# Cluster sums of an image from bf16 parts of x, and one product with ones per unit

## What is computed

```python
xn = x / max(norm(x, axis=1), EPS); cn = centroids / max(norm(centroids, axis=1), EPS)
idx = argmax(einsum('bchw,nc->bnhw', xn, cn), axis=1)
onehot = one_hot(idx, 40)
sum_x = einsum('bhwn,bchw->bnc', onehot, x)          # cluster sums of each image
count = sum(onehot, axis=(1, 2))
centroids_local = sum_x / maximum(count, 1.0)[..., None]
gathered = centroids_local[b, idx]                   # the mean of each position's cluster
delta = transpose(gathered) - x
alpha = exp(-mean(delta * delta, axis=1, keepdims=True))
y = x + alpha * delta
out = relu(einsum('oc,bchw->bohw', W, y) + b)
```

## Time and profile before

| | |
|---|---|
| median of 3 runs | 431.25 us (431.1 to 432.02) |
| the profiled execution | 431.4 us, span 429.6 us |
| TensorE (PE) busy | 422.2 us, 98% |
| VectorE (DVE) busy | 285.3 us, 66% |
| ScalarE (ACT) busy | 243.4 us, 57% |
| GpSimd (POOL) busy | 206.7 us, 48% |
| HBM | 48.40 MB read, 25.17 MB written |

### The profile page before, as it was taken

One profiled execution on the slowest core, in us unless ns is written; L12 is line 12 of the kernel. 1 busy time (PEld: TensorE's weight loads), 2 busy tenths in 40 slices (PEclk: granted clock), 3 DMA queues, 4 the chain that ended last, 5 costly groups with the idle time before them and its releaser, 6 DMA issues.

```text
span 429.6 us, 5789 instructions
## 1 busy us (share of the span) xinstructions
PE 422.2 (98%) x2134; PEld 296.0 (69%) x2134; DVE 285.3 (66%) x378; ACT 243.4 (57%) x329; POOL 206.7 (48%) x102
## 2 busy tenths in 40 slices
PE   8999999999999999999999999999999999999996
PEld 6744466775777667775867757776677758777785
DVE  2368979485776767495883857767674956787730
ACT  5665385566465673565754664656735657555541
POOL 2000665486284482674553862844826745424330
PEclk9999999999999999999999999999999999999999
DMA  8996298976577946859379665879463220222123
GB/s 275 309 291 122 56 261 219 274 218 166 143 244 185 226 168 164 215 149 256 99 198 265 169 175 142 242 182 229 163 170 125 98 99 0 98 99 98 49 112 134
DMA packets 70927, 73.94 MB, mean 172 GB/s; under 512 B 2724, under 2 KB 45732, under 8 KB 70900
## 3 DMA queue, kind: packets, MB, share of 16 engines
q1 hardware_dynamic: 70900, 73.58, 61.9%
HBM read 48.40 MB, written 25.17 MB: 171 GB/s over the span
## 4 chain that ended last, share of the span: by engine, by line
PE 95%; DVE 2%; ACT 1%; issue 1%; POOL 0%; POOLq 0%; DVEq 0%
PE main L797 20%; PE main L799 20%; PE main L798 20%; PE sump L740 10%; PE fa L700 9%; PE gat L771 5%; PE al L778 1%; PE fa L709 1%; PE al L779 1%; PE al L819 1%; PE fa L724 1%; PE main L840 1%; PE al L785 1%; PE gat L785 1%; PE gat L812 1%
## 5 line engine op out<-in xcount | busy, mean ns | idle before, releaser
L284 POOL TENSOR_TENSOR z<-z,x 128x1024 f32<-128x1024 f32 x42 | 99.3, 2384 | 147.1 <-DVE z L389 147.1
L797 PE MATMUL main<-yh,wh 128*128 128x512 f32 x376 | 152.5, 406 | 0.0
L799 PE MATMUL main<-yh,wl 128*128 128x512 f32 x376 | 147.0, 391 | 0.0
L798 PE MATMUL main<-yl,wh 128*128 128x512 f32 x376 | 146.7, 390 | 0.0
L291 POOL TENSOR_TENSOR yl<-z,yh 128x1024 fp32r<-128x1024 f32 x44 | 106.0, 2423 | 57.9 <-ACT yh L530 57.9
L369 DVE TENSOR_TENSOR z<-gat,x 128x1024 f32<-128x1024 f32 x46 | 56.2, 1221 | 91.1 <-PE gat L771 91.1
L538 ACT ACTIVATE o<-main,bcol 128x512 f32<-128x512 f32 x96 | 65.7, 686 | 82.8 <-PE main L799 82.8
L797 PEld LDWEIGHTS main<-yh,wh 128*128 128x128 f32 x376 | 70.7, 188 | 20.4 <-issue 4.6
L799 PEld LDWEIGHTS main<-yh,wl 128*128 128x128 f32 x376 | 70.6, 188 | 15.2
L798 PEld LDWEIGHTS main<-yl,wh 128*128 128x128 f32 x376 | 70.7, 188 | 14.3
L530 ACT ACTIVATE yh<-z 128x1024 fp32r<-128x1024 f32 x48 | 50.5, 1052 | 22.9 <-POOL z L284 21.9
(11 more groups left out here) (114 smaller groups left out, 325.5 us busy)
## 6 DMA issues: line engine op xcount, KB each, us to landing
x<-x SPq DMA_DIRECT2D x24, 1024.0 KB, 5.7
out<-o SPq DMA_DIRECT2D x23, 1024.0 KB, 4.8
xs<-x SPq DMA_DIRECT2D x84, 256.0 KB, 6.3
o<-w SPq DMA_DIRECT2D x1, 1024.0 KB, 12.3
out<-o SPq DMA_DIRECT2D x4, 256.0 KB, 2.1
sq<-centroids SPq DMA_DIRECT2D x2, 80.0 KB
bcol<-bias SPq DMA_DIRECT2D x1, 2.0 KB, 11.7
```

The lines of the kernel that those rows point to most:

```text
L284: pool.tensor_tensor(z, z, X[g // PARTS % 2][:, pair(h), span(g)], ALU.add).then_inc(y_pool, 1)
L797: t_.matmul(main[:, o % 2, :], WH[:, k, rows], YH[g % 2][:, k, :], start=(k == 0), stop=False)
L798: t_.matmul(main[:, o % 2, :], WH[:, k, rows], YL[g % 2][:, k, :], start=False, stop=False)
L799: last = t_.matmul(main[:, o % 2, :], WL[:, k, rows], YH[g % 2][:, k, :], start=False, stop=(k == KC - 1))
```

## The change

For images 2 to 7 (g >= 6), two of the three units of an image (g % 3 below SPLIT = 2) get their cluster sums in another way. x is written exactly as three bf16 parts: the upper halfword of XT; then GpSimd (`first_rest`) subtracts that from XT into a new buffer XR, whose upper halfword is the second part; VectorE (`second_rest`) subtracts this in turn and writes the result, in bf16, into XR's lower halfwords. TensorE takes 12 bf16 products with `oh3` in place of 4 float32 products with `oh`, so it waits for `oh3_done` and `rest2_done`. GpSimd issues `first_rest(g + 5)` after `low_half(g, 1)`, VectorE `second_rest(g + 3)` at the end of an iteration. The third unit and images 0 and 1 stay in float32.

The ones product becomes one: ScalarE copies the upper 64 partitions of `al` (`move_upper`), VectorE adds them to the lower 64 (`fold`), `high_sum` and `low_sum` work on 64 partitions and write the two halves of one buffer SHL, and TensorE multiplies it once. It now stands after the last block of convolve, ahead of the next gather, for every g (for g = 2 after a block of convolve); `exp(g - 1)` moves to the next iteration, behind `relu(g - 3, 3)`. `argmax` is cut into `best_sims` and `first_best`, `means` into `scale_means` and `high_means`, and the order of calls on VectorE and ScalarE changes around them. keep_busy goes from 9 to 6.

```diff
+def split(g):
+    return g >= 2 * PARTS and g % PARTS < SPLIT
...
+        XR = sb("xr", [P, SPLIT, TILES, C], F32)
...
-        SH = sb("sh", [P, UNIT], F32R)
-        SL = sb("sl", [P, UNIT], F32R)
+        upper_sum = sb("upper_sum", [LOW, UNIT], F32)
+        SHL = sb("shl", [P, UNIT], F32R)
...
+            def first_rest(g):
+                pool.wait_ge(tr_done, g - PARTS + 1)
+                xt = XT[:, g % PARTS, :, :]
+                pool.tensor_tensor(XR[:, g % PARTS, :, :].rearrange("p t c -> p (t c)"),
+                                   xt.rearrange("p t c -> p (t c)"), halfword(xt, 1), ALU.subtract
+                                   ).then_inc(rest1_done, 1)
...
                 low_half(g, 0)
                 low_half(g, 1)
+                if g + 5 < UNITS and split(g + 5):
+                    first_rest(g + 5)
...
+            def second_rest(g):
+                dve.wait_ge(rest1_done, splits(g))
+                xr = XR[:, g % PARTS, :, :]
+                v_.tensor_tensor(halfword(xr, 0), xr.rearrange("p t c -> p (t c)"), halfword(xr, 1), ALU.subtract
+                                 ).then_inc(rest2_done, 1)
...
+            def fold(g):
+                dve.wait_ge(upper_done, folded(g))
+                v_.tensor_tensor(al[0:LOW, :], upper_sum[:, :], al[0:LOW, :], ALU.add).then_inc(fold_done, 1)
...
                 add_squares(g)
-                if beside and p < 2:
+                if beside and p == 0:
                     transpose_half(g + 4, 1)
+                fold(g)
                 if beside and p == 2:
                     rest_of_mean(b + 1)
+                if beside and p == 1:
+                    best_sims(b + 1)
                 low_half(g - 1, 1)
                 low_sum(g)
                 if beside and p == 1:
-                    argmax(b + 1)
+                    first_best(b + 1)
+                    transpose_half(g + 4, 1)
                 if beside and p == 2:
                     parts_of_mean(b + 1)
                     if g + 4 < UNITS:
                         transpose_half(g + 4, 0)
                         transpose_half(g + 4, 1)
+                if g + 3 < UNITS and split(g + 3):
+                    second_rest(g + 3)
...
+            def move_upper(g):
+                act.wait_ge(s_done, folded(g))
+                a_.activation(upper_sum[:, :], al[LOW:P, :], ACT.Copy).then_inc(upper_done, 1)
...
                 b, p = divmod(g, PARTS)
                 beside = b + 1 < BATCH
+                relu(g - 3, 3)
                 if g > PARTS:
-                    relu(g - 3, 3)
+                    exp(g - 1)
                 square(g, 0)
...
                     high_half(g - 1, 1)
-                    means(b + 1)
                     relu(g - 2, 0)
+                    scale_means(b + 1)
+                    move_upper(g)
+                    high_means(b + 1)
                     high_sum(g)
                     relu(g - 2, 1)
...
+                    move_upper(g)
+                    high_half(g - 1, 1)
                     high_sum(g)
-                    high_half(g - 1, 1)
                     if beside:
                         relu(g - 2, 1)
                 relu(g - 2, 2)
-                exp(g)
                 if beside and p == 1:
                     copy_onehot(b + 1)
...
+                if split(PARTS * b + u):
+
+                    pe.wait_ge(oh3_done, b + 1)
+                    pe.wait_ge(rest2_done, splits(PARTS * b + u))
+                    for t in range(HALF):
+                        for i, x_part in enumerate((halfword(XT[:, u, :, :], 1), halfword(XR[:, u, :, :], 1),
+                                                    halfword(XR[:, u, :, :], 0))):
+                            for h in range(2):
+                                tile = HALF * h + t
+                                last = t_.matmul(sumP[NPAD * h:NPAD * (h + 1), :], oh3[:, slot(u, tile), 0:NPAD],
+                                                 x_part[:, tile * C:(tile + 1) * C],
+                                                 start=(u == 0 and t == 0 and i == 0), stop=False)
+                    last.then_inc(c_done, 1)
+                    return
...
-                t_.matmul(al[:, :], ones[:, :], SH[:, :], start=True, stop=False)
-                t_.matmul(al[:, :], ones[:, :], SL[:, :], start=False, stop=True).then_inc(one_done, 1)
+                t_.matmul(al[:, :], ones[:, :], SHL[:, :], start=True, stop=True).then_inc(one_done, 1)
...
-            keep_busy(9)
+            keep_busy(6)
...
                 convolve(g - LAG, 2)
-                if beside:
-                    sum_squares(g)
                 convolve(g - LAG, 3)
-                if not beside:
-                    sum_squares(g)
+                sum_squares(g)
```

More of the change, by code:

```diff
@@ L31 @@
 LAG = 2
+LOW = P // 2
 EPS = 1e-12
 TAIL = UNITS - 1 - PARTS
+SPLIT = 2
 DIRECT = 2
@@ L57, in made, with splits @@
     return by_vector, 2 * g + h + 1 - by_vector
+def split(g):
+    return g >= 2 * PARTS and g % PARTS < SPLIT
+def splits(g):
+    return sum(split(i) for i in range(g + 1))
 def folded(g):
@@ L153, in build @@
         pair_done, s_done, sh_done, sl_done = sem("pair_done"), sem("s_done"), sem("sh_done"), sem("sl_done")
+        rest1_done, rest2_done = sem("rest1_done"), sem("rest2_done")
+        upper_done, fold_done = sem("upper_done"), sem("fold_done")
         one_done, exp_done, za_done = sem("one_done"), sem("exp_done"), sem("za_done")
@@ L180, in squares, with halfword @@
             return SQ[:, :, :] if h == 0 else gat[:, :, :]
+        def halfword(words, which):
+            return words.rearrange("p t c -> p (t c)").bitcast(BF16).rearrange("p (c w) -> p c w", w=2)[:, :, which]
         def plain(b):
@@ L317, in transpose_half, with best_sims @@
                     last.then_inc(tr_done, 1)
-            def argmax(b):
-                shape = [P, PARTS * TILES, N]
+            def second_rest(g):
[3 more added lines that the diff above has]
+                                 ).then_inc(rest2_done, 1)
+            def best_sims(b):
                 dve.wait_ge(simT_done, b + 1)
@@ L323, in argmax, with first_best @@
                 v_.tensor_reduce(best[:, :], simT, AXIS_X, ALU.max).then_inc(arg_step, 1)
+            def first_best(b):
+                shape = [P, PARTS * TILES, N]
                 dve.wait_ge(arg_step, 4 * b + 1)
@@ L379, in add_squares @@
                 v_.tensor_tensor(al[:, :], SQ[:, 0, :], upper[:, 1, :], ALU.add).then_inc(s_done, 1)
+            def fold(g):
+                dve.wait_ge(upper_done, folded(g))
+                v_.tensor_tensor(al[0:LOW, :], upper_sum[:, :], al[0:LOW, :], ALU.add).then_inc(fold_done, 1)
             def low_sum(g):
                 dve.wait_ge(sh_done, folded(g))
-                wait(dve, one_done, g)
-                v_.tensor_tensor(SL[:, :], al[:, :], SH[:, :].bitcast(F32), ALU.subtract).then_inc(sl_done, 1)
+                v_.tensor_tensor(SHL[LOW:P, :], al[0:LOW, :], SHL[0:LOW, :].bitcast(F32), ALU.subtract
+                                 ).then_inc(sl_done, 1)
             def scale(g, h):
@@ L431, in _ @@
             keep_transposed()
-            argmax(0)
+            best_sims(0)
+            first_best(0)
             for k in range(KC):
@@ L444, in _ @@
                 delta(g, 1)
-            argmax(1)
+            best_sims(1)
+            first_best(1)
             scale(0, 0)
@@ L461, in _ @@
             rest_of_mean(1)
+            parts_of_mean(1)
+            fold(2)
             low_sum(2)
-            parts_of_mean(1)
             transpose_half(6, 0)
@@ L567, in copy_sums, with scale_means @@
                 a_.activation(sumsH[:, :], sumP[:, :], ACT.Copy).then_inc(sumsH_done, 1)
-            def means(b):
+            def scale_means(b):
                 act.wait_ge(rc_step, 2 * b + 2)
@@ L572, in means, with high_means @@
                 a_.activation(mean(b), mean(b), ACT.Copy, scale=rcount[:, :]).then_inc(mean_step, 1)
+            def high_means(b):
                 act.wait_ge(mean_step, 2 * b + 1)
@@ L607, in _ @@
             evacuate_onehot(0)
-            means(0)
+            scale_means(0)
+            high_means(0)
             act.wait_ge(b_in, 16)
@@ L628, in _ @@
             square(2, 1)
-            means(1)
+            scale_means(1)
+            high_means(1)
+            move_upper(2)
             high_half(1, 1)
@@ L632, in _ @@
             relu(0, 2)
-            relu(0, 3)
-            exp(2)
             for g in range(PARTS, UNITS):
@@ L652, in _ @@
                     relu(g - 2, 0)
+                    if g == PARTS:
+                        exp(g - 1)
                     square(g, 1)
@@ L670, in _ @@
             relu(g - 2, 3)
+            exp(g)
             relu(g - 1, 0)
@@ L894, in _ @@
             convolve(0, 3)
-            sum_squares(2)
             for g in range(PARTS, UNITS):
@@ L908, in _ @@
                     convolve(g - LAG, 0)
```

(4 more changed lines are left out.)

4 lines of the change are left out of this document (2 added, 2 removed).

## The result

The changed kernel takes 435.03 us (434.76 to 435.35, 4 runs) against 431.63 us before it on the same chip: ratio 1.0076, 95% interval 1.0062 to 1.0091. It is slower by 3.4 us, where I had forecast 7.3; the sign is right and the size is not. The profiled execution took 435.28 us with a span of 433.5 us, 3.9 longer than before.

What follows compares the result with a forecast made beforehand. TensorE's work was taken as the bound: 431.4 - 10.8 saved + 17.1 of stalls (6 images x 2.85) + 1.1 for the first iteration = 438.8, or 438.6 at the median; own range 434 to 444, 8-in-10 range 422 to 445.

Steps and rivals of the forecast that it cites:

- What bounds the kernel: TensorE, busy 98% of the span; from 70 us on, time is the sum of its work, other engines in its shadow.
- Part 1, the ones product: On TensorE, 22 units keep one ones product of a pair: 5.1 us less, 0.69 an image.
- Part 2, bf16 pairs side by side: In TensorE's cluster sums, six bf16 pairs take 1.35 us a split unit, 0.44 less: 5.3 us over 12 units.
- keep_busy, 0.4: Three keep_busy products fewer on TensorE were worth 0 to 1.3 us, taken as 0.4.
- Part 3: Added work elsewhere: GpSimd's subtractions 4.7 us each (bounds 3.5 and 6), VectorE's 2.3, plus 22 folds and 22 copies.
- Unit p = 1: VectorE's second_rest ends at t 17.2, the next unit's first delta starts at t 2.3, not 0.64; sums wait 0.5 us.
- unit p = 2: The late delta brings the count at t 10.4; TensorE waits 1.0 us at add_halves; an image gains 1.57, gives 1.5 back.
- Unit p = 0, and the port: GpSimd and VectorE exclude each other; GpSimd reaches y_half of p = 1 at t 5.5, not 3.1: stalls 2.85 us an image.
- My own sign of being wrong: A GpSimd subtraction of much under 4.7 us would break the squeeze of p = 0.
- The first iteration: At the main loop's start, relu 1 of unit 3 comes up to 2.2 us late; bounds 0 and 2.2, taken 1.1.
- the port does no harm: Second rival: first_rest of p = 2 lands before t 3.1 of the next unit; 1.5 us an image remain, 429 to 433; chance 0.20.

Runs made afterwards that it cites:

- e6: Changed kernel with one split unit an image from image 3, second in order behind a float32 unit, and unit 3's calls reordered (relus ahead of waiting sums): 424.3 us.
- e1: Changed kernel with no split: all cluster sums in float32, the single ones product and other moves kept: 429.84 us, ratio 0.9962.
- e2: Changed kernel with TensorE taking the float32 unit of an image first, then the two bf16 units: 435.11 us, ratio 1.0085.
- e3: Changed kernel without VectorE's second remainder in p = 1; TensorE takes the second part twice, its work unchanged: 428.39 us, ratio 0.993.
- e8: Changed kernel with GpSimd's first_rest taking XT in float32 as both operands: 435.34 us, ratio 1.0092.
- e9: Changed kernel with first_rest's operands written as 4 tiles of 512 channels, not one flat run of 2048: 434.58 us, ratio 1.007.
- e12: Changed kernel with GpSimd's first_rest issued as two subtractions over 128x1024 instead of one over 128x2048: 435.04 us, ratio 1.0097.
- e7: e1 (no split) with unit 3's calls reordered as in e6: 426.17 us, ratio 0.9878.
- e10: Changed kernel with GpSimd's low_half given its operands as flat runs of 1024 instead of (2, 512): 434.64 us, ratio 1.0071.
- e11: e6 with nine keep_busy products at the start instead of six: 425.34 us, ratio 0.9846.

## Why the prediction was wrong in size, point by point

- What bounds the kernel: right. Without waits the time is TensorE's work; e6, almost without them, shows it.
- Part 1, the ones product, 0.69 an image: right. e1's images are 0.76 shorter.
- Part 2, bf16 pairs side by side at 1.35 us a unit: right. Unit 1's products start at 153.57 and the next unit's at 154.97, 1.40 us. Without waits the sums take 4.58 us in e2 (201.13 to 205.71) and 5.30 in e1 (199.01 to 204.31), so two units save 0.72 (0.88 forecast). keep_busy, 0.4: not seen, and no run shows it.
- Part 3, VectorE's remainder 2.3 us: it takes 2.56 alone. GpSimd's, 4.7 us with bounds of 3.5 and 6: it takes 3.60, inside the bounds, but the rest went by 4.7 alone.
- Unit p = 1 and unit p = 2, the chain from second_rest to add_halves: right. The first delta came at 2.65 (2.3 forecast), the count ended at 211.28, 10.4 into its unit, as forecast (the row is below); being held costs TensorE 1.5, as forecast: 1.0 at the sums (6.36 us for 5.36, see e2; the two waits listed there are 0.20 and 0.52) and the other 0.5 at add_halves (0.27 of wait listed). Their shares differ: I had no wait for the weights, where 0.20 was met, 0.5 at the sums in all and 1.0 at add_halves. The total held because the late count sets it. e2 and e3 show that chain and that second_rest starts it. ScalarE's timeline of the changed kernel, to be set beside the earlier trace rows:

```profile
211.07 0.21 ACT L617 ACTIVATION_READ_ACCUMULATOR oht<-fa 128x1 f32 x1
```

- **The step that failed is the squeeze in "Unit p = 0, and the port".** It made 2.85 us of stalls an image out of 1.5, and 17.1 in six images; measured are 6 x 1.53 = 9.2. The exclusion was right (4.62 us for 2.56 alone, 5.96 for 3.60), and so was VectorE's place ahead of GpSimd's next instruction, which the forecast counted on without a row and the changed kernel shows in six images (183.75 in the one above). The price of GpSimd's subtraction, 4.7 us, was not: at 3.60, twice, GpSimd has 2.2 us more, and y_half of p = 1 starts at t 3.6, not 5.5. My own sign of being wrong, a subtraction of much under 4.7 us, is what came. Whether 4.7 us would have led to images of 51.4 was not tested, since e8, e9 and e12 never reached that price; the slack of 1.25 us in p = 1 says that a wait of about 0.6 would have started there (an estimate).
- The first iteration, 1.1 us taken between 0 and 2.2: it cost 3.84, outside the bounds. I had followed GpSimd's queue and left out ScalarE's: relu(0,2) behind high_sum(2), and square(3,0) with its late delta ahead of exp(2). This error of 2.7 us hid a third of the other, 7.9: that the time came within 3.6 us of the forecast is in part luck.
- With the right stalls my sum is 431.4 - 10.8 + 9.2 + 3.8 = 433.6, and the 1.4 us of too much gain (1.0 in the pairs' saving, 0.4 for keep_busy) make 435.0; 435.28 was measured, and 0.2 of the rest lies ahead of the first gather (33.96 us for 33.75).
- The rivals: the second, "the port does no harm", is what happened in the images; its time, 429 to 433, missed the start. Its reason is not: first_rest of p = 2 lands at t 4.2 of the next unit (174.34), after the 3.1 that it names, and y_half of p = 0 does start 1.1 us later than before; it costs nothing.

## What to carry to other kernels

When an engine is full and another engine's work is taken in to relieve it, the price is paid where that work stands in the other engine's queue, not by its share of busy time: 2.56 us of VectorE in p = 1 cost 1.15 us an image, the same instruction in p = 0 nothing (15.87 us with it in e6, 15.87 without in e7). Waits that follow from one late instruction are one loss; test with a reordering (e2) before counting them as several. And look at the first iteration by itself: relus behind sums that wait, and an exp behind a square that waits, cost 3.8 us there where an image cost 0.06, and the cure was an order.

## What the runs showed of the hardware

- GpSimd's tensor_tensor over 128x2048 took 3.60 us alone, and 1.9 over 128x1024, when both operands were the same words; over two tiles 128x1024 took 2.4. Neither the type of the remainder's operand (e8, 3.60) nor the form (e9, 3.60; e10, 2415 ns for 2416) changed that.
- VectorE with two SBUF operands, having asked during a GpSimd instruction, ran at that instruction's end and ahead of GpSimd's next one (183.75), in all six images of the changed kernel (its six second_rests of p = 0 take 3.55 to 4.66 us, GpSimd's next instruction 5.96 to 5.99), and so in e12 (3.55 to 4.77 us, and 6.12 to 6.14 for the two GpSimd instructions that take 3.75 alone). The same rows show the exclusion: 4.62 us for a 2.56 us operation, and 5.96 for 3.60.
- TensorE's first similarities took 2.60 us in the changed kernel and 2.44 in e11 where they took 1.95 before, at a recorded clock of 1.00. With six keep_busy products it is 1.95 (e9) to 2.66 (e6), so their number doesn't decide it, and nothing here says what does.
